# Router logits of a mixture-of-experts stage with the gate as TensorE's stationary operand

## What is computed

```
router_logits = jax.nn.sigmoid(x @ gate_w + gate_b)
expert_values, expert_indices = jax.lax.top_k(router_logits, k=TOP_K)
expert_values = expert_values / jnp.sum(expert_values, axis=-1, keepdims=True)
```

## Time and profile before

| | us |
|---|---|
| median of 3 runs | 1973.44 |
| lowest and highest of them | 1964.8, 1974.52 |
| the profiled execution, its time | 1971.4 |
| its span, first to last instruction | 1969.7 |
| mean granted clock of TensorE, share of full speed | 0.929 |

### The profile page before, as it was taken

One profiled execution on the slowest core, in us unless ns is written; L12 is line 12 of the kernel. 1 busy time (PEld: TensorE's weight loads), 2 busy tenths in 40 slices (PEclk: granted clock), 3 DMA queues, 4 the chain that ended last, 5 costly groups with the idle time before them and its releaser, 6 DMA issues. The chain is left out here.

```text
span 1969.7 us, 33146 instructions
## 1 busy us (share of the span) xinstructions
PE 1683.1 (85%) x9122; PEld 1161.0 (59%) x9123; DVE 1194.9 (61%) x4117; ACT 1010.2 (51%) x2504; POOL 546.9 (28%) x680
## 2 busy tenths in 40 slices
PE   6899989898998999979509993789999998689997
PEld 4656666666665666667307772456656665356675
DVE  1886858686868686825104453478888877403445
ACT  1774747475757475723203334366667765554331
POOL 2001010101000010100750006978889873300001
PEclk9999999999899999986759995689999999899999
DMA  5212121211103020200223442688787776010000
GB/s 123 62 39 70 37 64 38 70 38 51 51 19 88 16 86 21 75 1 1 93 101 120 135 133 70 126 140 138 137 135 133 122 121 103 7 44 16 22 17 32
DMA packets 92015, 142.62 MB, mean 72 GB/s; under 512 B 15872, under 2 KB 48080, under 8 KB 91760
## 3 DMA queue, kind: packets, MB, share of 16 engines
q1 hardware_dynamic: 78512, 106.41, 25.8%
q0 software_dynamic: 11648, 34.25, 6.0%
q10 hardware_dynamic: 1728, 0.55, 0.2%
HBM read 73.52 MB, written 50.33 MB: 63 GB/s over the span
## 5 line engine op out<-in xcount | busy, mean ns | idle before, releaser
L137 ACT ACTIVATE a_prob<-a_prob,a_negmax 128x128 f32<-128x128 f32 (+3 forms) x512 | 279.6, 551 | 0.0
L1624 ACT ACTIVATE a_probT<-a_ps_st 128x384 f32<-128x384 f32 (+1 forms) x384 | 189.7, 526 | 135.1 <-PE a_ps_st L1497 130.1
L127 DVE CUSTOM_DVE_ANT_0 a_prob<-a_ps_score,c_mask 128x128 f32<-128x128 f32 (+3 forms) x512 | 221.2, 486 | 34.4 <-PE a_ps_score L433 17.3
L1735 DVE CUSTOM_DVE_ANT_0 a_junk<-a_ps_score,c_mask 128x128 f32<-128x128 f32 (+3 forms) x512 | 220.4, 486 | 35.1 <-PE a_ps_score L1475 28.1
L175 ACT ACTIVATE a_probT<-a_ps_trans 128x512 f32<-128x512 f32 (+1 forms) x256 | 124.7, 487 | 225.0 <-PE a_ps_trans L163 224.0
L163 PE MATMUL a_ps_trans<-c_ident,a_prob 128*128 128x128 f32 x1280 | 195.2, 285 | 40.5 <-DVE a_prob L147 26.6
L163 PEld LDWEIGHTS a_ps_trans<-c_ident,a_prob 128*128 128x128 f32 x1280 | 149.6, 144 | 113.8 <-issue 51.7
L616 POOL TENSOR_SCALAR a_rstd<-a_mv 128x4 f32<-128x4 f32 x8 | 1.8, 221 | 769.4 <-DVE a_mv L608 769.4
L432 PE MATMUL a_ps_score<-a_kh,a_qs 128*128 128x128 f32 (+3 forms) x512 | 168.7, 353 | 24.2 <-DVE a_negmax L127 16.3
L1333 POOL TENSOR_TENSOR a_ms<-a_ms,c_minus_half 128x16 f32<-128x16 f32 x64 | 187.6, 2933 | 0.7 <-issue 0.6
L1497 PE MATMUL a_ps_st<-a_qs,a_ks 128*128 128x512 f32 (+3 forms) x512 | 154.6, 364 | 22.8 <-ACT a_probT L1624 11.7
(11 more groups left out here) (206 smaller groups left out, 3127.9 us busy)
## 6 DMA issues: line engine op xcount, KB each, us to landing
a_qs<-a_qlow SPq DMA_DIRECT2D x128, 128.0 KB, 2.2
bounce<-a_words SPq DMA_DIRECT2D x64, 256.0 KB, 2.0
a_qs<-bounce SPq DMA_DIRECT2D x128, 128.0 KB, 5.7
a_ks<-bounce SPq DMA_DIRECT2D x128, 128.0 KB, 6.1
slot_in<-es_zero POOLq DMA_DIRECT2D x16, 640.0 KB, 7.2
m_z<-slot_in SPq DMA_DIRECT2D x80, 128.0 KB, 2.1
slot_out<-m_y SPq DMA_DIRECT2D x80, 128.0 KB, 1.7
a_xT<-in_xT SPq DMA_DIRECT2D x8, 512.0 KB, 3.6
```

Source lines behind the costliest of these rows:

```text
L127: dve.tensor_tensor_reduce(out=self.prob[:, h % 4, QOFF[i]:QOFF[i] + keys], in0=self.ps_score[g][:, at:at + keys], in1=self.C.mask[:, L - ...
L137: act.activation(at, at, ACT.Exp, scale=-1.0, bias=self.negmax[:, h % 4, i:i + 1], accum_out=self.rowsum[:, h % self.ring, i:i + 1]).then_ ...
L1624: act.activation(probT[:, r8, col:col + width], ps_st[item % 2][:, 0:width], ACT.Exp).then_inc(s_stc, 1)
L1735: dve.tensor_tensor_reduce(out=junk[:, to:to + keys], in0=ps_score[g][:, at:at + keys], in1=C.mask[:, L - keys:L], scale=-1.0, scalar=3.0e ...
```

## The change

The logits are made the other way round. The gate (128 by 16 for each half of the features) is the stationary operand, and 512 tokens move past it, so a group needs 2 products instead of 8, and the logits come out with the 16 experts on the partitions and 512 tokens in a row. The bias now lies on the partitions too and goes into ScalarE's sigmoid, which reads PSUM and writes 16 by 512 values to the first 16 rows of a buffer of the shared expert (`gact`). A new step on TensorE, `back(g)`, turns these with 4 small transposes (16 by 128 each) into `ps_d`, tokens on the partitions, and VectorE takes its maxima and indices straight from there. VectorE's `biased` is gone. `back(g - 1)` follows `gate(g)`; `back(7)` stands ahead of `up(0)`. On ScalarE `keep(g + 1)` now comes ahead of `squash(g)`.

```diff
--- before.py
+++ after.py
@@ -687,7 +687,7 @@
         self.wgu = S.sb("wgu", [P, E, KT * 2 * I])
         self.wd = S.sb("wd", [I, E, D])
         self.shared_gu, self.shared_d = S.sb("shared_gu", [P, KT, 2, I]), S.sb("shared_d", [I, D])
-        self.gate, self.bias = S.sb("gate", [P, KT, E]), S.sb("bias", [P, E])
+        self.gate, self.bias = S.sb("gate", [P, KT, E]), S.sb("bias", [E, 1])
         self.iota, self.tiota = S.sb("iota", [P, E]), S.sb("tiota", [P, NS])
         self.before = S.sb("before", [P, P])
         self.thr = S.sb("thr", [P, 32])
@@ -737,7 +737,6 @@
         wgu, wd = ES.shared_gu, ES.shared_d
         ones = S.sb("ones", [P, P])
         xs = S.sb("xs", [P, KT, NT * P])
-        sig = S.sb("sig", [P, NT, E])
         top = S.sb("top", [P, NT, 8])
         tidx = S.sb("tidx", [P, NT, 8], U32)
         idx = S.sb("idx", [P, NT, 2])
@@ -755,11 +754,12 @@
         gact = [S.sb(f"gact{j}", [I, GL]) for j in range(2)]
         lin = [S.sb(f"lin{j}", [I, GL]) for j in range(2)]
         hid = [S.sb(f"hid{j}", [I, GL]) for j in range(2)]
+        sig = [gact[j][0:E, :] for j in range(2)]
         ps_turn = [S.ps(f"ps_turn{k}") for k in range(KT)]
         ps_g = [S.ps("ps_g0"), S.ps("ps_g1")]
         ps_u = [S.ps("ps_u0"), S.ps("ps_u1")]
         ps_d = [S.ps("ps_d0"), S.ps("ps_d1")]
-        s_turn, s_xs, s_gate, s_biased, s_sig = (S.sem(n) for n in ("turn", "xs", "gate", "biased", "sig"))
+        s_turn, s_xs, s_gate, s_sig, s_back = (S.sem(n) for n in ("turn", "xs", "gate", "sig", "back"))
         s_ones, s_v, s_count, s_rank, s_slot = (S.sem(n) for n in ("ones", "v", "count", "rank", "slot"))
         s_gu, s_silu, s_lin, s_hid, s_hid_late, s_down, s_kept, s_scatter = (
             S.sem(n) for n in ("gu", "silu", "lin", "hid", "hid_late", "down", "kept", "scatter"))
@@ -816,13 +816,20 @@
                 def gate(g):
                     pe.wait_ge(s_xs, KT * (g + 1))
                     if g >= 2:
-                        pe.wait_ge(s_biased, g - 1)
+                        pe.wait_ge(s_sig, g - 1)
+                    for k in range(KT):
+                        last = pe.matmul(ps_g[g % 2][0:E, :], ES.gate[:, k, :], xs[:, k, g * GL:(g + 1) * GL],
+                                         start=k == 0, stop=k == KT - 1)
+                    last.then_inc(s_gate, 1)
+
+                def back(g):
+                    pe.wait_ge(s_sig, g + 1)
+                    if g >= 2:
+                        pe.wait_ge(s_count, g - 1)
                     for t in range(GT):
-                        at = P * (g * GT + t)
-                        for k in range(KT):
-                            last = pe.matmul(ps_g[g % 2][:, E * t:E * (t + 1)], xs[:, k, at:at + P],
-                                             ES.gate[:, k, :], start=k == 0, stop=k == KT - 1)
-                    last.then_inc(s_gate, 1)
+                        last = pe.transpose(ps_d[g % 2][:, E * t:E * (t + 1)], sig[g % 2][:, P * t:P * (t + 1)],
+                                            C.ident[0:E, 0:E])
+                    last.then_inc(s_back, 1)
 
                 def up(g):
                     j = g % 2
@@ -830,7 +837,7 @@
                         pe.wait_ge(s_silu, g - 1)
                         pe.wait_ge(s_lin, g - 1)
                     else:
-                        pe.wait_ge(s_biased, NG - 1 + g)
+                        pe.wait_ge(s_sig, NG - 1 + g)
                     for c, ps in enumerate((ps_g[j], ps_u[j])):
                         for k in range(KT):
                             last = pe.matmul(ps[:], wgu[:, k, c, :], xs[:, k, g * GL:(g + 1) * GL],
@@ -860,6 +867,9 @@
                     if g + 1 < NG:
                         turn(g + 1)
                     gate(g)
+                    if g >= 1:
+                        back(g - 1)
+                back(NG - 1)
                 up(0)
                 ranks()
                 up(1)
@@ -876,8 +886,10 @@
                         act.activation(xs[:, k, g * GL:(g + 1) * GL], ps_turn[k][:], ACT.Copy).then_inc(s_xs, 1)
 
                 def squash(g):
-                    act.wait_ge(s_biased, g + 1)
-                    act.activation(sig[:, tiles_of(g), :], sig[:, tiles_of(g), :], ACT.Sigmoid).then_inc(s_sig, 1)
+                    act.wait_ge(s_gate, g + 1)
+                    if g >= 2:
+                        act.wait_ge(s_back, g - 1)
+                    act.activation(sig[g % 2], ps_g[g % 2][0:E, :], ACT.Sigmoid, bias=bias[:, 0:1]).then_inc(s_sig, 1)
 
                 def parts(g):
                     j = g % 2
@@ -894,11 +906,11 @@
                         act.activation(base[:, g * GT + 2 * c:g * GT + 2 * c + 2, :],
                                        ps_d[c][:].rearrange("p (t d) -> p t d", d=D), ACT.Copy).then_inc(s_kept, 1)
 
+                keep(0)
                 for g in range(NG):
-                    keep(g)
-                    if g >= 1:
-                        squash(g - 1)
-                squash(NG - 1)
+                    if g + 1 < NG:
+                        keep(g + 1)
+                    squash(g)
                 parts(0)
                 parts(1)
                 for g in range(NG):
@@ -916,21 +928,18 @@
                     ins.then_inc(s_v, 1)
                     dve.wait_ge(s_v, done[0])
 
-                def biased(g):
-                    dve.wait_ge(s_gate, g + 1)
-                    dve.tensor_tensor(sig[:, tiles_of(g), :],
-                                      ps_g[g % 2][:, 0:GT * E].rearrange("p (t e) -> p t e", e=E),
-                                      bias[:].unsqueeze(1).to_broadcast([P, GT, E]), ALU.add).then_inc(s_biased, 1)
+                def score(g, t):
+                    return ps_d[g % 2][:, E * (t % GT):E * (t % GT + 1)]
 
                 def choose(g):
                     at = tiles_of(g)
-                    dve.wait_ge(s_sig, g + 1)
+                    dve.wait_ge(s_back, g + 1)
                     for t in range(g * GT, (g + 1) * GT):
-                        dve.max(top[:, t, :], sig[:, t, :]).then_inc(s_v, 1)
+                        dve.max(top[:, t, :], score(g, t)).then_inc(s_v, 1)
                     done[0] += GT
                     dve.wait_ge(s_v, done[0])
                     for t in range(g * GT, (g + 1) * GT):
-                        dve.max_index(tidx[:, t, :], top[:, t, :], sig[:, t, :]).then_inc(s_v, 1)
+                        dve.max_index(tidx[:, t, :], top[:, t, :], score(g, t)).then_inc(s_v, 1)
                     done[0] += GT
                     dve.wait_ge(s_v, done[0])
                     do(dve.tensor_copy(idx[:, at, :], tidx[:, at, 0:2]))
@@ -946,10 +955,7 @@
                 dve.wait_ge(ES.s_small, ES.small)
                 dve.memset(ones[:], 1.0).then_inc(s_ones, 1)
                 for g in range(NG):
-                    biased(g)
-                    if g >= 1:
-                        choose(g - 1)
-                choose(NG - 1)
+                    choose(g)
                 dve.wait_ge(s_rank, 1)
                 tot = ps_turn[0][:].rearrange("p (t e) -> p t e", e=E)
                 rank = ps_turn[1][:].rearrange("p (t e) -> p t e", e=E)
@@ -2013,7 +2019,7 @@
         "wqT": i[a0 + "Wq"].transpose(2, 1, 0), "wkT": i[a0 + "Wk_up"].transpose(2, 1, 0),
         "wvT": i[a0 + "Wv_up"].transpose(2, 1, 0), "wo": i[a0 + "Wout"].transpose(1, 0, 2),
         "wdn": i[a0 + "Wkv_down"],
-        "gate_w": i[f0 + "gate_w"], "gate_b": np.broadcast_to(i[f0 + "gate_b"], (P, E)),
+        "gate_w": i[f0 + "gate_w"], "gate_b": i[f0 + "gate_b"].reshape(E, 1),
         "swg": i[f0 + "shared_wg"], "swu": i[f0 + "shared_wu"], "swd": i[f0 + "shared_wd"],
         "ewg": i[f0 + "experts_wg"], "ewu": i[f0 + "experts_wu"], "ewd": i[f0 + "experts_wd"],
         "wdq": eight(i[a1 + "W_DQ"]), "wuqT": eight(i[a1 + "W_UQ"].T),
```

## The result

| | before | changed |
|---|---|---|
| median, us (runs) | 1969.75 (5) | 1955.10 (5) |
| lowest and highest | 1964.8, 1974.52 | 1952.12, 1955.97 |
| ratio, 95% interval | | 0.992, 0.9897 to 0.9944 |
| profiled execution, its span | 1971.4, 1969.7 | 1955.1, 1953.0 |
| mean granted clock | 0.929 | 0.939 |

The change makes the kernel 14.65 us faster (11 to 20 by the interval). The forecast was 12.7 us slower; what happened is rival A, the clock that rises.

The account below looks back on a forecast made before the run. TensorE at the lower clock was taken as the bound of the gate stage; 1.0 + 6.7 + 5.0 = +12.7 us on 1971.4 gave 1984.1, shifted by 2.0 to 1986. The range was 1957 to 1992.

Parts of the forecast that it names:

- rival A: TensorE's clock rises in the gate stage because fed rows, or any 512-column stream, count: -13.9 us, 1959.5; chance 0.35.
- The clock: TensorE in the gate stage: filled array cells count, 128*16 weights fill an eighth, so the granted clock stays at 0.50.
- Gate products: TensorE, lower clock: four 512-column passes take 3.40 us a group against 3.28, +1.0 us over 8 groups.
- Transposes back: TensorE: 32 small transposes at 0.21 us each, +6.7 us; bounds +3.4 and +11.8.
- Changes of shape: TensorE: switching array shape, 8 changes at 0.11 and 14 at 0.29, +5.0 us; bounds 0 and twice that.
- forecast case: Clock stays low in the gate stage with about the forecast costs: +12.7 us; chance 0.57.
- wait of back(7) for its sigmoid: Last transposes back wait for squash(7): 0 to 0.3 us, taken as 0; about 0.4 in the rising-clock case.
- The last two choices: VectorE: choose(6) and choose(7) take 3.9 us after back(6); at the risen clock they fit just so.
- VectorE from PSUM: VectorE's choices now read PSUM: nothing added, still 1.96 us a group.
- The stretch behind up(0): From up(0) through slots to scatters: no slack, so a gate end moved by x moves all that follows by x.
- transposes count toward the rise: TensorE: read from layer 0 attention, where the clock rose after 1.75 us of transposes and 1.2 us of 512-column matmuls.

Follow-up runs that it names:

- x1: Changed kernel with each gate product fed only the first 64 of its 128 rows: 1979.39 us, 8.3 above before (1971.07).
- x2: Changed kernel with 64 rows by 128 columns of the shared expert's weights in place of the gate's: 1980.54 us (+9.5).
- x3: Changed kernel with each gate product fed 96 of its 128 rows: 1951.98 us (-19.1, one execution).
- x8: Kernel of before with four added 512-column passes over 128 rows ahead of each group's gate, result unused: 1970.4 us against 1974.58, ratio 0.9974.
- x9: Changed kernel with each small transpose back issued twice: 1957.57 us.
- x6: Changed kernel with three instead of four of the shared expert's elementwise products on GpSimd (fourth to VectorE): 1954.0 us, ratio 0.9894.
- x10: Kernel of before with the second halves of up(0) and up(1) moved ahead of gates 0 and 1: 1965.5 us against 1972.18, ratio 0.9952.
- x12: Kernel of before with the second halves of up(0) and up(1) moved ahead of gates 0 and 4: 1957.67 us against 1970.41, ratio 0.9933.

## Why the prediction was wrong

**The clock: failed.** The step was "If cells count, it will leave the clock low ... I take cells". x1, x2 and x3 decide against cells: a stream over 64 rows leaves the clock at 0.50 whether it fills 16 columns or 128, a stream over 96 or 128 rows raises it with 16. With the rows counted in place of the cells the step would have forecast the higher level. The reasoning from the earlier trace rows used two changes at once. The array's first work had both half the rows and half the cells; my reason spoke only against columns alone and the mere presence of a matmul; it gave nothing against rows, which the same paragraph named. What the earlier trace rows show fits too: the old form feeds 128 rows, but for 16 columns a pass between loads of 128, and the clock stayed low from a low start. So rows alone don't do it either; x8 shows that long passes added to the old form do. The Trainium skill (TensorE: Matmul & The Clock Gate, Part 1) ties the higher clock to sustained matmul activity. Its outcome for the change was the right one. x1 doesn't agree with it: TensorE is busy for 47.37 us of 47.60 and the clock stays at 0.50.

**Gate products: right.** 3.52 us a group at the lower level (x1) with its change of shape; forecast 3.40 + 0.11. At the higher level it is 1.82 (888.53 to 890.35).

**Transposes back: too dear.** Forecast 0.21 a step by the old steps, with half of it as the lower bound. x1 has 0.53 us from the first of four to the next turn, a change of shape included: 0.107 a step and 0.10 for the change. At the higher level x9 gives 0.062. These steps with a 16*128 load take about half of those with a 128*128 load (0.213 and 0.107); the lower bound was the value.

**Changes of shape: too dear.** Forecast 0.69 a group (0.11, 0.29, 0.29). The 5.95 us of x1 less 8 x 0.213, 4 x 0.853 and 4 x 0.107 leave 0.41; the 3.19 of the change less 8 x 0.107, 4 x 0.427 and 4 x 0.062 leave 0.38. So at the lower clock, where the sum had +12.7, x1 measured +7.2. The forecast case was 5.5 us too slow by its prices alone, apart from the clock.

**Rival A: right in its mechanism, near in each number.**

| | rival A | measured |
|---|---|---|
| first transpose to up(0), us | 29.4 | 28.52 |
| up(0) to the rank products | 3.4 | 3.54 |
| a group | 3.4 | 3.19 |
| wait of back(7) for its sigmoid | 0.4 | 0.42 |
| total against before | -13.9 | -14.64 in the stage, -14.65 in the medians |

That the sum is so near is partly luck. Rival A took over the prices that were too dear (6.7 us a group at the lower level, 5.95 in x1), and it halved all of them for the higher clock, which was too much: the changes of shape hardly shrink (0.41 to 0.38), and 5.95 became 3.19 and not 2.98. The two errors offset.

The last two choices ended at 909.67, 0.33 us ahead of the rank products: they fit just so. By the runs, the gain is the sum of two terms: +7.2 for the new form (x1 less before) and 50.95 - 72.8 = -21.9 for the clock (the change less x1).

**VectorE from PSUM: right, nothing.** MAX8 takes 0.42 us for four where the earlier trace rows have 0.39, the whole choice 2.01 against 1.96. The Trainium skill (VectorE: DVE Perf Modes, on the errata) gives VectorE a fixed cost that is 62 cycles larger for a PSUM source, an estimate of 0.5 us a group; 0.05 was measured.

**The stretch behind up(0): not without slack.** Before, the slots were ready at 937.16 (936.97 and 0.19), while GpSimd's fourth product ran to 939.70:

```profile
937.39 2.31 POOL L786 TENSOR_TENSOR mr_hid<-mr_gact,mr_lin 128x512 f32<-128x512 f32 x1 [3.89 <-ACT mr_lin L889]
```

Both hang on up(0), so the whole still moved with it, but the slots had 2.5 us to spare, and x6 uses most of that.

**Not covered.** That the clock outlasts the streams, by 11.8 us in x10 and by 9.3 and 9.1 in x12, was in no case; it didn't bear on the change, which streams in every group. That transposes count toward the rise, as the prediction read from the earlier trace rows, was not tested by itself.

**The shares.** Rival A had 0.35, the forecast case 0.57. The earlier trace rows gave no ground for more than even odds between rows and cells; by the prices now measured that is a coin with a loss of 7 and a gain of 14 us.

## What to carry to other kernels

Where TensorE is the bound, read its granted clock before counting its passes: here a form that is dearer at either level won, because it streams 512 columns over all 128 rows in every group. Before rewriting such a stage for the clock, try to move long streams that the kernel needs anyway into it (x12: two half products moved, within the interval of the whole change), and spread them: with both at the start (x10) the clock fell for the last third of the stage, and the median was only 6.7 us below before. And price a rival's mechanism by separating its variables: a row that differs in two of them decides nothing between the two.

## What was unexpected of the hardware

- Streams over 64 rows (64*16 and 64*128 weights, 512 columns) leave the granted clock at 0.50 while TensorE is busy for 47.37 of 47.60 us (x1) and for 48.97 of 49.20 (x2); over 96 or 128 rows with 16 columns of weights it was 1.00 from about 5 us after the stage's first transpose.
- Passes that by themselves didn't raise the clock in 40 us kept it, once up, for 11.8 us after the last stream in x10, and for 9.3 and 9.1 us in x12. In x10 the time of one and the same kernel spread over 1950.35 to 1973.07; that the moment of the fall makes this spread was not shown, since one execution has a profile.
- A small transpose with a 16*128 load follows the next after 0.107 us at the lower level and 0.062 at the higher one, where those with 128*128 take 0.213 and 0.107.
